# Graph attention over 64 tiles on one core: the second phase turns its exponentials by blocks, on VectorE and GpSimd, in place of two TensorE products per step

## The reference, cut to what matters

```python
u = einsum('bid,bjd->bij', h, h) / sqrt(D)
a = softmax(u, axis=-1)
delta = a * adjacency_matrix
attn = delta / (sum(delta, axis=-1) + 1e-10)
hl, hs, hr = h @ wl.T + b_l, h @ ws.T + b_s, h @ wr.T + b_r
ctx = (attn * upper) @ hl + diag(attn) * hs + (attn * lower) @ hr
o = relu((ctx - mean(ctx)) / sqrt(var(ctx) + eps) * g + beta)
```

## Time and profile before

| | |
|---|---|
| median of 3 runs | 1207.33 us |
| the profiled execution | 1207.23 us |
| its span in the trace | 1205.4 us |
| TensorE busy | 1195.3 us, 99% |
| VectorE busy | 1075.5 us, 89% |
| ScalarE busy | 986.5 us, 82% |
| GpSimd busy | 388.6 us, 32% |
| chain that ended last | TensorE 96%, VectorE 2%, DMA 1%, issue 1% |

### The profile page before, as it was taken

One profiled execution on the slowest core, in us unless ns is written; L12 is line 12 of the kernel. 1 busy time (PEld: TensorE's weight loads), 2 busy tenths in 40 slices (PEclk: granted clock), 3 DMA queues, 4 the chain that ended last, 5 costly groups with the idle time before them and its releaser, 6 DMA issues.

```text
span 1205.4 us, 26740 instructions
## 1 busy us (share of the span) xinstructions
PE 1195.3 (99%) x7010; PEld 1185.4 (98%) x7010; DVE 1075.5 (89%) x2924; ACT 986.5 (82%) x2673; POOL 388.6 (32%) x665
## 2 busy tenths in 40 slices
PE   8999999999999999999999999999999999999997
PEld 7999999999999999999999999999999999999997
DVE  7999999999988888888888888999999999999986
ACT  7888888888777788888888988888888788888874
POOL 2333334343332212122121121234343444434342
PEclk9999999999999999999999999999999999999999
DMA  6434334342422233433333233322332323332321
GB/s 212 130 105 132 117 101 122 96 124 86 124 72 97 85 103 106 131 109 112 116 102 112 94 99 110 112 80 89 101 106 98 109 98 109 98 97 99 98 92 55
DMA packets 112994, 127.64 MB, mean 106 GB/s; under 512 B 11136, under 2 KB 100224, under 8 KB 112896
## 3 DMA queue, kind: packets, MB, share of 16 engines
q1 hardware_dynamic: 112896, 126.50, 33.2%
HBM read 76.91 MB, written 49.55 MB: 105 GB/s over the span
## 4 chain that ended last, share of the span: by engine, by line
PE 96%; DVE 2%; DMA 1%; issue 1%; ACT 0%; SPq 0%; POOLq 0%; POOL 0%; DVEq 0%; ACTq 0%
PE left_bank L504 25%; PE right_bank L504 24%; PE context_bank L504 24%; PE context_bank L538 17%; PE score_bank L480 5%; DMA vector_rows<-vectors 1%; DVE in_stats L881 0%; DMA squares<-turned 0%; DVE side_parts L1011 0%; DVE stats L1016 0%; PE edge_bank L494 0%; PE edge_bank L488 0%; DVE weight L999 0%; DVE rows L1065 0%; DVE turned L898 0%
## 5 line engine op out<-in xcount | busy, mean ns | idle before, releaser
L504 PE MATMUL left_bank<-weight,node_t 128*128 128x384 f32 x1728 | 337.4, 338 | 0.4 <-DVE weight L999 0.4
L504 PE MATMUL right_bank<-weight,node_t 128*128 128x384 f32 x1728 | 333.3, 337 | 0.0
L504 PE MATMUL context_bank<-weight,node_t 128*128 128x384 f32 x1728 | 330.8, 336 | 0.0
L504 PEld LDWEIGHTS left_bank<-weight,node_t 128*128 128x128 f32 x1728 | 303.7, 188 | 0.7 <-DVE weight L999 0.7
L504 PEld LDWEIGHTS context_bank<-weight,node_t 128*128 128x128 f32 x1728 | 302.4, 188 | 0.0
L504 PEld LDWEIGHTS right_bank<-weight,node_t 128*128 128x128 f32 x1728 | 298.7, 188 | 0.0
L538 PE MATMUL context_bank<-side_parts,attn_t 128*128 128x386 f32 x1152 | 238.2, 342 | 1.9 <-issue 1.0
L1283 POOL TENSOR_TENSOR rstd<-spread,scalars 128x2 f32<-128x2 f32 x95 | 71.2, 749 | 436.7 <-DVE spread L1034 432.7
L538 PEld LDWEIGHTS context_bank<-side_parts,attn_t 128*128 128x128 f32 x1152 | 200.3, 189 | 8.5 <-issue 4.0
L698 ACT ACTIVATE side_parts<-right_bank 128x384 fp32r<-128x384 f32 x192 | 94.4, 492 | 112.5 <-PE context_bank L538 112.4
L902 DVE TENSOR_TENSOR node_t<-nodes,node_t 128x768 fp32r<-128x768 f32 x94 | 151.0, 1606 | 1.3 <-ACT node_t L631 0.9
(11 more groups left out here) (92 smaller groups left out, 1657.3 us busy)
## 6 DMA issues: line engine op xcount, KB each, us to landing
squares<-turned SPq DMA_DIRECT2D x94, 384.0 KB, 2.7
nodes<-squares SPq DMA_DIRECT2D x376, 96.0 KB, 2.2
rows<-x SPq DMA_DIRECT2D x63, 384.0 KB, 4.0
out<-rows SPq DMA_DIRECT2D x31, 384.0 KB, 2.6
adj_in<-adj SPq DMA_DIRECT2D x96, 64.0 KB, 1.9
piece<-weights SPq DMA_DIRECT2D x18, 192.0 KB, 2.5
rows<-weights SPq DMA_DIRECT2D x2, 576.0 KB, 8.4
vector_rows<-vectors SPq DMA_DIRECT2D x3, 384.0 KB, 4.9
```

The lines of the kernel that those rows point to most:

```text
L504: mm = nc.tensor.matmul(bank[:, 0:D], node_t[:, s.parity, k, c, a], weight[:, s.phase % 2, w, c, b], start=False, stop=(c, a) == (CH - 1, ...
```

## The change

In phase 1 the cross is added by blocks, as in the other phases (`by_blocks` no longer asks for `bounded`), so `turn_cross` runs only in the first three steps of the kernel. The maximum is no longer spread: `place_max`, `spread_max`, `shift_scores` and `totals` go. ScalarE makes the exponentials by row once, with the bias and the sum, into a new tile `exps`. VectorE transposes its 32x32 blocks twice, into `score` and into `exps_turned_here` (`turn_exps`), and GpSimd moves the off-diagonal blocks of the second into `score` in four instructions (`move_exps`). `mask_edges` waits for these and stands at the head of the next body. `place_edges` goes to the head of the next body on GpSimd, `spreads` and the square before it go ahead of the scores' sum, and `diagonal` and one `split_piece` move. Phase 2 has its `gather_input` a little earlier. The last step gets an order of its own on TensorE, ScalarE and VectorE.

```diff
@@ by_blocks, block_index
-    return s.bounded and not (isinstance(s.n, int) and s.n < FIRST_BY_BLOCKS)
+    return not (isinstance(s.n, int) and s.n < FIRST_BY_BLOCKS)
...
-    return s.normal - FIRST_BY_BLOCKS
+    return s.n - FIRST_BY_BLOCKS
@@ TensorE
-            def spread_max(s):
-                pe.wait_ge(max_placed, s.n + 1 - PAIRS)
-                nc.tensor.matmul(edge_bank[:, 0:2 * NODES], same_graph[:, :], max_diag[:, :, :].rearrange("p k i -> p (k i)"),
-                                 start=True, stop=True).then_inc(max_spread, 1)
...
+            def weigh_last(s, k):
...
+                for side in (RIGHT, LEFT):
+                    pe.wait_ge(side_hi[side], s.tile(k) + 1)
+                    for a, b in ((HI, HI), (LO, HI), (HI, LO)):
+                        if b == LO:
+                            pe.wait_ge(side_lo[side], s.tile(k) + 1)
...
+            def last_step(s):
+                prev = s.ahead(-1)
+                project_side(s, 0, RIGHT)
+                weigh(prev, 1)
+                project_self(s, 0)
+                project_side(s, 0, LEFT)
+                project_side(s, 1, RIGHT)
+                weigh(s, 0)
+                project_self(s, 1)
+                project_side(s, 1, LEFT)
+                weigh_last(s, 1)
...
-                project_side(s, 1, LEFT, within=(lambda: spread_max(nxt)) if nxt.exists() and not nxt.bounded else None)
+                project_side(s, 1, LEFT)
@@ ScalarE
-            def totals(s):
...
                 if not s.bounded:
-                    act.wait_ge(shift_done, s.n + 1 - PAIRS)
-                    nc.scalar.activation(score[:, :, :], score[:, :, :], ACT.Exp, scale=SCALE).then_inc(exp_done, 2)
+                    act.wait_ge(max_bias_done, s.n + 1 - PAIRS)
+                    act.wait_ge(den_done, s.tile(0) - 2)
+                    for k in range(2):
+                        nc.scalar.activation(exps[:, k], score[:, k], ACT.Exp, bias=max_bias[:, k:k + 1], scale=SCALE,
+                                             accum_out=total[:, s.parity, k:k + 1]).then_inc(exp_done, 1)
...
-                if s.phase == 2 and prev.level():
+                if prev.level():
                     square(prev, 1)
...
                 split_side(s, 1, LEFT)
-                if nxt.exists() and not nxt.bounded:
-                    exponentials(nxt)
+                if s.phase == 1:
+                    scale_self(s, 1)
                 if nxt.exists():
                     seed_side(nxt, 0, LEFT)
@@ VectorE
+            def turn_exps(s):
+                dve.wait_ge(exp_done, 2 * s.n + 2)
+                for turned_exps in (score, exps_turned_here):
+                    nc.vector.transpose(turned_exps[:, :, :].rearrange("p k j -> p (k j)"),
+                                        exps[:, :, :].rearrange("p k j -> p (k j)")).then_inc(exps_turned, 1)
...
-                diagonal(s)
+                if s.bounded:
+                    diagonal(s)
+                else:
+                    mask_edges(s)
...
                 split_side(s, 0, RIGHT)
+                if not s.bounded:
+                    diagonal(s)
...
-                if s.phase == 2 and prev.level():
+                if prev.level():
                     spreads(prev)
+                if s.phase == 2 and fourth.exists():
+                    gather_input(fourth, 0)
+                    gather_input(fourth, 1)
                 if nxt.exists():
                     sum_scores(nxt)
...
-                if s.phase == 2:
...
+                norm(prev, 0)
+                if s.phase > 0:
                     split_side(s, 1, RIGHT)
                     if nxt.exists():
                         turn_blocks(nxt)
...
                     row_maximum(nxt)
-                    place_max(nxt)
+                    negate_max(nxt)
...
                 denominator(s, 0)
+                if nxt.exists() and not nxt.bounded:
+                    turn_exps(nxt)
...
-                if nxt.exists() and not nxt.bounded:
-                    mask_edges(nxt)
                 split_side(s, 1, LEFT)
@@ GpSimd
+            def move_exps(s, fourth):
+                pool.wait_ge(exps_turned, 2 * (s.n + 1 - PAIRS))
+                if fourth.exists() and fourth.bounded:
+                    pool.wait_ge(in_rstd_done, fourth.normal + 1)
...
+                for q in range(QUARTERS):
+                    r, here, other = q % 2, q * Q, (q ^ 1) * Q
+                    at_least(pool, exps_placed, QUARTERS * (s.n - PAIRS) + q)
+                    ones = vector_rows[other:other + Q, 0, 5 * D:5 * D + 1].unsqueeze(2).to_broadcast([Q, 2, Q])
+                    nc.gpsimd.tensor_tensor(placed[here:here + Q, :, 1 - r], copied[other:other + Q, :, r], ones, ALU.mult)\
+                      .then_inc(exps_placed, 1)
...
-                if s.phase == 1 and nxt.exists() and by_blocks(nxt):
+                if not s.bounded:
+                    place_edges(s)
+                output_rstd(prev)
+                if nxt.exists() and by_blocks(nxt):
                     move_blocks(nxt)
...
-                if nxt.exists():
+                if nxt.exists() and nxt.bounded:
                     place_edges(nxt)
+                if nxt.exists() and not nxt.bounded:
+                    move_exps(nxt, fourth)
```

More of the change, by code:

```diff
@@ L812, in first_steps, with last_step @@
                 exponentials(s2)
+            def last_step(s):
+                prev = s.ahead(-1)
+                square(prev, 0)
+                seed_self(s, 0)
+                seed_side(s, 1, RIGHT)
+                split_side(s, 0, RIGHT)
+                split_edges(s)
+                square(prev, 1)
+                scale_self(s, 0)
+                split_side(s, 0, LEFT)
+                seed_side(s, 1, LEFT)
+                seed_self(s, 1)
+                split_side(s, 1, RIGHT)
+                scale_self(s, 1)
+                split_side(s, 1, LEFT)
             def body(s):
@@ L839, in body @@
                 seed_side(s, 1, LEFT)
-                if s.phase < 2 and prev.exists() and prev.level():
-                    square(prev, 1)
                 if len(pieces) > 0:
@@ L1140, in first_steps, with finish_tile, last_step @@
                 centre(s1, 0)
+            def finish_tile(s, k):
+                denominator(s, k)
+                context_stats(s, k)
+                last_squared(s, k)
+                gather_moments(s, k)
+                last_spread(s, k)
+                centre(s, k)
+            def last_step(s):
+                prev = s.ahead(-1)
+                diagonal(s)
+                denominator(prev, 1)
+                squared_denominator(prev)
+                centre(prev, 1)
+                split_side(s, 0, RIGHT)
+                split_edges(s)
+                spreads(prev)
+                split_side(s, 0, LEFT)
+                norm(prev, 0)
+                residual(prev, 0)
+                norm(prev, 1)
+                split_side(s, 1, RIGHT)
+                residual(prev, 1)
+                finish_tile(s, 0)
+                norm(s, 0)
+                split_side(s, 1, LEFT)
+                residual(s, 0)
+                finish_tile(s, 1)
+                norm(s, 1)
+                residual(s, 1)
             def body(s):
@@ L1166, in body @@
                     input_stats(fourth, 1)
-                if s.phase == 0 and len(averaged) > 0:
+                if len(averaged) > 0:
                     split_piece(*averaged[0])
@@ L1181, in body @@
                     input_stats(fourth, 1)
-                if nxt.exists() and by_blocks(nxt) and s.phase < 2:
+                if s.phase == 0 and by_blocks(nxt):
                     turn_blocks(nxt)
-                if prev.exists() and not prev.level():
-                    norm(prev, 0)
-                if s.phase == 2:
-                    if fourth.exists():
-                        gather_input(fourth, 0)
-                        gather_input(fourth, 1)
-                    norm(prev, 0)
+                norm(prev, 0)
+                if s.phase > 0:
                     split_side(s, 1, RIGHT)
@@ L1203, in body @@
                     gather_input(fourth, 1)
-                if s.phase == 1 and len(averaged) > 0:
-                    split_piece(*averaged[0])
-                if s.phase == 2:
+                if s.phase == 0:
+                    split_side(s, 1, RIGHT)
+                if prev.phase > 0:
                     residual(prev, 0)
-                elif s.phase == 0:
-                    split_side(s, 1, RIGHT)
-                else:
-                    split_side(s, 1, RIGHT)
-                    if prev.level():
-                        norm(prev, 0)
-                    if nxt.exists() and not nxt.bounded:
-                        shift_scores(nxt)
-                    if prev.phase > 0:
-                        residual(prev, 0)
                 if prev.exists():
@@ L1260, in _ @@
             walk(dve, body)
```

(8 more changed lines are left out.)

112 lines of the change are left out of this document (43 added, 69 removed).

## The result

The changed kernel takes 1209.49 us (median of 18 runs, 1209.09 to 1210.57) against 1206.98 us (18 runs, 1206.60 to 1207.48) for the kernel before on the same chip: 1.0022 times as long, 95% interval 1.0015 to 1.0028. It is slower by 2.5 us. The forecast was slower by 6.7 us: the sign was right and the size was not, being 2.7 times too large. The profiled execution took 1209.09 us, with a span of 1207.3 us.

What follows compares the result with a forecast made beforehand. VectorE's queue between tile 1's splits, against a window set by TensorE's pace, bounds phase 1: 32 x 12.60 plus 1.7 and 2.5 gives +7.7, the end -1.0, so 1213.9 us; range 1199 to 1225, the forecast's own 1209 to 1218.

Steps and rivals of the forecast that it cites:

- The window in phase 1: VectorE's queue between tile 1's RIGHT and LEFT splits: 4.57 us in 4.20, 0.37 late, 12.60 us a step.
- The steps with extra work: Phase 1, VectorE's first half: nine weight-piece steps cost 1.7 us in all, the last three with input statistics 2.5 us.
- Phase 2: Only `gather_input` moves, into VectorE's wait for ScalarE's copies: no change, bound 1.6 us to both sides.
- The end: Last step: final weighing earlier and statistics following at once, 1.0 us off, bounds 0 and 1.6.
- A: Phase 1: VectorE's window fits, TensorE sets steps of 12.22 us, kernel 1197.6 us; chance 0.18.
- C: Phase 1: L902 loses its race, keeps 1.83 us, GpSimd's loop sets 12.8 us steps, kernel 1225 us; chance 0.16.
- D: Phase 1: squared denominator waits for both GpSimd mask instructions, loop of 13.4 us, kernel 1244 us; chance 0.07.
- B: Phase 1: window overrun only 0.1 to 0.25 us, less first-half loss; kernel 1205 to 1209.6 us; chance 0.12.

## Why the prediction was wrong in size, point by point

**The window in phase 1** was right, term by term. Forecast: RIGHT split at +4.14, 4.57 us of queue, LEFT split's end at +8.71, 0.37 us late, 12.60 us a step. Measured: +4.13, 4.55, +8.68, 0.34 (the weighing's 1.55 against 1.21), 12.57. Thirty-two times 0.03 is 1.0 us of the miss. That the window decides is shown by three runs: +0.29 us a step for a transposition inside, nothing for the same behind it, -0.35 for a residual taken out.

**The steps with extra work** were put at 1.7 us for the weight pieces and 2.5 for the last three. The piece steps cost nothing: they stand among the plain steps at 12.57. The slack ahead of the block transposition was 0.5 us and not 0.3, since the four moves start at +2.37 and take 1.73 us. Behind a split piece they start at +2.62, as forecast some 0.2 us later, and take 1.58: still 0.4 us ahead of the transposition at +4.60. The last three steps did cost, 13.0 each, and so did two kinds that the forecast didn't have: the three with bias rows (12.94, 12.94, 13.30) and the four of the hardware loop (12.82). The first two steps took 0.6 us less than plain ones. In sum it was 3.2 us and not 4.2; that the costs forecast and the costs left out nearly cancel is luck. The loop's share can be read in its window:

```profile
718.42 0.16 DVE L961 SCALAR_TENSOR_TENSOR max_bias<-row_max,scalars 128x2 f32<-128x2 f32 x1
718.75 0.56 DVE L1087 SCALAR_TENSOR_TENSOR rows<-context,rows 128x384 f32 x1 [0.17 <-issue]
```

From the negation to the residual are 0.33 us there and 0.08 in the written-out steps, and the 0.25 us are the whole difference between 12.82 and 12.57. The likely reason is that in the loop the values to wait for have to be computed; no run tested it. In the kernel before, the loop's steps take 12.48 to 12.50 us against 12.47, so there it hardly showed.

**Phase 2** is the step that failed: "In phase 2 only `gather_input` moves ...: nothing, with 0.05 us per step, 1.6 us, as the bound to both sides." It is -2.6 us. I had measured that phase 2 ran at +8.44 for the LEFT split, 0.10 late, with a wait of 0.24 for GpSimd ahead of the transposition, and used that to find the threshold for phase 1, but didn't ask what would become of those 0.10 themselves. I had even taken 1.76 us as what GpSimd's four moves cost; it holds a collision in it. The move of `gather_input` was priced at nothing because it went into a wait; in the kernel before it is worth 2.2 us by itself. In the changed kernel the same 2.6 us come without it too, so what was left out is more than one edit: it is that phase 2 could leave its 12.32 us at all. Of the 4.2 us by which the time was missed (1213.9 against 1207.2 + 2.5), phase 2 is 2.6, and phase 1 is 2.0 (7.7 forecast, 5.7 measured), the mis-sized terms being the plain step and the extras above; the rest, -0.4, is that the medians differ by 2.5 us where the profiled spans differ by 1.9, and small change.

**The end** was put at -1.0 us and is -1.0.

**The rivals.** A (TensorE at its own pace) didn't come with the change, but its price is nearly what the residual's move gives: 12.22 us plain steps and 1200.5 us instead of 1197.6, and 1197.9 with the statistics moved too. C: L902 won its race, 0.95 us. The loop doesn't decide: VectorE waits in no plain step for the moves ahead of the block transposition. D: the squared denominator got in between GpSimd's two instructions, at 0.24 us instead of 0.16. B is near what came: the kernel's 0.22% lies just above its edge, though by another way, an overrun of the full size and a gain in phase 2.

What stays open: which entry to phase 2 leads to 12.32 us and which to 12.22, why the kernel before slides into the slower one over its first five steps, and what makes VectorE pause in the two kernels with a third transposition.

## What to carry to other kernels

An in-order queue has to be held against the window between two events that the bounding engine sets, not against the length of the step: VectorE with 17% of idle time in phase 1 made TensorE wait 0.34 us in every step, and one instruction moved behind the deadline, into a wait that was there anyway, turned 2.5 us lost into 7 us gained. When a product is taken from the bounding engine, the windows that lay over it shrink as well, and what replaces it must not stand in them. And where a trace shows a small stall or a collision in a phase that the change hardly touches, price its disappearance too.

## What the runs showed of the hardware

Which of VectorE and GpSimd starts first decides what both take when each reads two SBUF operands. The 128x768 subtraction takes 0.95 us when it starts first and GpSimd's 128x128 multiply then 1.11 instead of 0.46; started 0.29 us into GpSimd's 128x512 multiply it takes 1.83, and 0.46 into it 1.66, ending 0.8 us after it in both. The Trainium skill, SBUF — State Buffer, "SBUF: two separate sides", has this as an exclusive lock held for the instruction, and these runs agree. The same holds for a shorter pair: a 128x384 norm that starts just ahead of GpSimd's second 32x64 move makes that move last 0.65 us instead of 0.29, and one that starts behind it lasts 0.63 to 0.70 us itself instead of 0.59. A waiting VectorE instruction got in between two GpSimd instructions that follow without a wait: the squared denominator, 0.24 us.

Two programs with the same order in a phase settled at different step times in it: 12.32 us in the kernel before, 12.22 in the changed kernel with the moved statistics put back. How they enter the phase is the difference that the traces show.

VectorE can lose time at one place of its program with no wait recorded, in one kernel and not in another with the same order there: 0.43 us once and then 0.19 instead of 0.08 in every second step of phase 2, in the two kernels with one transposition more in phase 1. A difference of 1 us between two kernels can come from that, and not from the edit's own cost.
